# Attention scores in two strips of 64 rows, taken two units at a time

## What is computed

```
x = x + 0.5 * ffn(layernorm(x))        # top 2 of 8 experts, hidden width 352
x = x + attn(layernorm(x))             # 16 heads of 8 features
x = x + 0.5 * ffn(layernorm(x))

attn:  q, k, v = x @ qkv_w.T;  q, k = rope(q), rope(k)
       s = q @ k.T * 8 ** -0.5 + min(key - query, 0) * slope[head] * 8
       out = (softmax(s) @ v) @ proj_w.T + proj_b
```

## Time and profile before

| | |
|---|---|
| median of 3 runs | 501.61 us (497.75 to 501.74) |
| the profiled execution | 502.36 us, of which the span is 500.5 us |
| mean granted TensorE clock | 0.972 |
| busy share of PE, PEld, DVE, ACT, POOL | 88%, 73%, 64%, 50%, 47% |
| shares of the chain that ended last | PE 58%, DVE 8%, issue 7%, ACT 5%, POOL 4%, DMA 3% |

### The profile page before, as it was taken

The page is one execution under the profiler, slowest core; times in us unless marked ns, Lnnn a source line. Parts: engine busy times, 40 slices in busy tenths (PEclk is TensorE's granted clock), DMA queues, the critical chain, the costliest instruction groups (busy, mean ns, idle before and its releaser), DMA issues.

```text
span 500.5 us, 10906 instructions
## 1 busy us (share of the span) xinstructions
PE 439.6 (88%) x3447; PEld 367.2 (73%) x3447; DVE 318.6 (64%) x935; ACT 249.1 (50%) x585; POOL 236.9 (47%) x321
## 2 busy tenths in 40 slices
PE   1999989989889884998989898989788999999990
PEld 1878878888878663676867676767557988888880
DVE  3767869778556645384868585847436675545672
ACT  4745644364443534354565546454664554554441
POOL 7267796564523214034435253514254568643341
PEclk9999999999999989798999899999998999999996
DMA  9981121223220102121212111110022123223522
GB/s 245 284 116 55 48 75 45 79 71 97 70 60 24 43 22 54 33 65 34 55 53 54 45 48 40 45 43 22 7 87 64 53 67 112 59 60 96 149 79 79
DMA packets 50633, 35.51 MB, mean 71 GB/s; under 512 B 5754, under 2 KB 47706, under 8 KB 50538
## 3 DMA queue, kind: packets, MB, share of 16 engines
q1 hardware_dynamic: 45140, 23.90, 19.3%
q0 software_dynamic: 4784, 10.54, 6.3%
q10 hardware_dynamic: 656, 0.40, 0.3%
HBM read 15.37 MB, written 13.01 MB: 57 GB/s over the span
## 4 chain that ended last, share of the span: by engine, by line
PE 58%; DVE 8%; issue 7%; ACT 5%; POOL 4%; DMA 3%; ACTq 1%; SPq 1%; POOLq 0%; DVEq 0%
PE bank L1582 6%; PE bank L1485 5%; PE bank L1606 5%; PE bank L1621 5%; PE bank L1478 5%; PE bank L1467 4%; PE bank L1468 3%; PE bank L1469 3%; PE bank L1585 3%; PE bank L1586 3%; PE bank L1609 2%; PE bank L1610 2%; POOL yp L538 2%; PE bank L1457 2%; DVE nm L1260 2%
## 5 line engine op out<-in xcount | busy, mean ns | idle before, releaser
L538 POOL DMA_INDIRECT yp<-scr,dest x77 | 76.5, 994 | 90.2 <-ACT scr L768 63.1
L1260 DVE TENSOR_REDUCE nm<-bank 128x2 f32<-128x512 f32 x128 | 83.9, 685 | 46.6 <-PE bank L1586 45.1
L875 ACT ACTIVATE stage<-bank 128x512 f32<-128x512 f32 x128 | 75.2, 596 | 68.8 <-PE bank L1610 68.1
L1485 PE MATMUL bank<-wd,scr 128*128 (+1 forms) x462 | 64.2, 275 | 1.3 <-ACT scr L761 1.3
L1467 PE MATMUL bank<-wu,xbT 128*128 x154 | 62.3, 405 | 2.1 <-DVE xbT L1126 1.8
L1134 DVE COPY scr<-bank 128x256 f32<-128x256 f32 x77 | 32.5, 423 | 46.8 <-PE bank L1478 46.3
L1485 PEld LDWEIGHTS bank<-wd,scr 128*128 128x128 f32 (+1 forms) x462 | 60.0, 191 | 1.8 <-issue 1.7
L1582 PE MATMUL bank<-qk_rows 126*128 126x256 bf16 x256 | 51.4, 283 | 5.5 <-DVE nm L1260 5.5
L1606 PE MATMUL bank<-qk_rows 128*128 128x256 bf16 x256 | 50.9, 282 | 2.4 <-DMA qk_rows<-wd 2.0
L781 ACT ACTIVATE scr<-bank 128x352 f32<-128x352 f32 x77 | 35.7, 464 | 32.4 <-PE bank L1469 32.1
L1469 PE MATMUL bank<-wu,xbT 128*128 x154 | 50.2, 326 | 0.0
(11 more groups left out here) (218 smaller groups left out, 958.7 us busy)
## 6 DMA issues: line engine op xcount, KB each, us to landing
qk_rows<-lev SPq DMA_DIRECT2D x96, 64.0 KB
scr<-xs SPq DMA_DIRECT2D x77, 64.5 KB, 1.9
stage<-yp SPq DMA_DIRECT2D x8, 256.0 KB, 4.1
scr<-yp SPq DMA_DIRECT2D x6, 256.0 KB, 2.9
stage<-in_w SPq DMA_DIRECT2D x8, 176.0 KB, 3.7
stage<-in_v SPq DMA_DIRECT2D x8, 176.0 KB, 5.1
xs<-qk_rows SPq DMA_DIRECT2D x3, 451.5 KB, 11.1
yp<-scr,dest POOLq DMA_INDIRECT x77
```

The lines of the kernel that those rows point to most:

```text
L538: nc.gpsimd.indirect_dma_start(out=yp[PHASE[n]][:, :], out_offset=bass.IndirectOffsetOnAxis(ap=dest[:, n:n + 1], axis=0), in_=ysb[:, n % Y ...
L875: nc.scalar.activation(probs[:, g % RING, kt, 2 * (hp % 2):2 * (hp % 2) + 2, :], psS2[(b * 16 + j) % 3][:, :].rearrange("p (h n) -> p h n" ...
L1260: nc.vector.tensor_reduce(nm[:, qt, 2 * hp:2 * hp + 2], psS1[i % 2][:, :].rearrange("p (h n) -> p h n", h=2), AX.X, ALU.max, negate=True). ...
L1485: i = nc.tensor.matmul(ph[n % len(ph)][:, 3 * P:4 * P], hTs[0:w, n % 2, k * P:(k + 1) * P], wd[0:w, bass.ds(experts[n], 1), k, :].rearrang ...
```

## The change

The 62 to 64 meaningful rows are now packed at a step of 8 into a strip of 64 partitions. Even heads lie in rows 0 to 63, odd heads in rows 64 to 127, so `qs` and `ks` hold 8 heads a strip, side by side in one tile. `scores_1` and `scores_2` are called for two units at once: unit i is the lower strip, unit i+1 the upper one, in two PSUM banks, and their products alternate. The near triangle is contracted over 64 rows too, which needs a part 128 wide and a part 64 wide for each of high and low (`near`). `STRIP` is 64, `NEAR` is 192. The two units together have 12 products where they had 8.

```
-S1_SLOTS = [1, 1, 2, 2, 0, 1, 1, 2, 2, 2, 1, 1, 0, 0, 0, 0]
-S1_LATE = [0, 0, 0, 1, 1, 1, 2, 2, 2, 2, 2, 2, 1, 0, 0, 0]
+S1_SLOTS = [2, 0, 2, 2, 0, 2, 2, 0, 2, 2, 0, 2, 0, 0, 0, 0]
+S1_LATE = [0, 0, 0, 2, 0, 2, 2, 0, 2, 2, 2, 2, 2, 0, 0, 0]
...
+            def near(o, i, c, col):
+                for parts in (near_hi, near_lo):
+                    for half in range(2):
+                        w = slice(half * P, P + half * STRIP)
...
+                        for strip in range(2):
+                            rows = slice(strip * STRIP, (strip + 1) * STRIP)
+                            m = nc.tensor.matmul(o[strip]..., idn_r[rows, to:to + P], parts[i][rows, 2 * c:2 * c + 2, w], ...)
...
             def scores_1(b, i):
...
                 if i >= 2:
-                    pe.wait_ge(max_found, b * 16 + i - 1)
-                o = psS1[i % 2]
-                for j in range(2):
-                    h = 2 * hp + j
-                    nc.tensor.matmul(o[:, j * N:(j + 1) * N], qs[b % RING][0:S1_ROWS, h, ...],
-                                     ks[b % RING][0:S1_ROWS, h, :], start=(j == 0), stop=False)
+                    pe.wait_ge(max_found, b * 16 + i)
+                for a in range(2):
+                    for strip in range(2):
+                        rows = slice(strip * STRIP, strip * STRIP + S1_ROWS)
+                        nc.tensor.matmul(psS1[strip][:, a * N:(a + 1) * N], qs[b % RING][rows, 2 * c + a, ...],
+                                         ks[b % RING][rows, 2 * c + a, :], start=(a == 0), stop=False)
+                near(psS1, 0, c, qt * P)
...
             def scores_2(b, j):
-                if n >= 3:
-                    pe.wait_ge(exp_done, n - 2)
-                o = psS2[n % 3]
+                if n >= 2:
+                    pe.wait_ge(exp_done, n - 1)
+                o = [psS2[(n + strip) % 3] for strip in range(2)]
```

The calls: PE makes a pair of `scores_2` units at every even slot and a pair of `scores_1` units at the slots with a 2. The maxima are split on DVE ahead of the transposes; ACT makes one copy and issues its two transfers one after the other, ahead of `ln2`:

```
-            def max_low(b):
-                dve.wait_ge(ml_hi, b + 1)
-                nc.vector.tensor_tensor(ml[:, 1, :], psS1[0][0:H, 0:N], ml[:, 0, :], ALU.subtract)
+            def max_split(b):
+                dve.wait_ge(max_found, b * 16 + 16)
+                nc.vector.tensor_copy(nm_hi[:, :, :], nm[:, :, :])
+                dve.wait_ge(nm_step, 3 * b + 1)
+                nc.vector.tensor_copy(nm_parts[:, :, 0, :], nm_hi[:, :, :])
+                nc.vector.tensor_tensor(nm_parts[:, :, 1, :], nm[:, :, :], nm_hi[:, :, :], ALU.subtract)
...
+            def max_rows(b):
+                act.wait_ge(mT_full, b + 1)
+                nc.scalar.activation(ml, psS1[0][0:2 * H, 0:N], copy)
+                act.wait_ge(ml_done, b + 1)
+                for strip in range(2):
+                    at = strip * STRIP + S1_ROWS
+                    act.dma_start(qs[b % RING][at:at + 2, :, :], ml[strip::2, :])
```

More of the change, by code:

```diff
@@ L489, in stack @@
-            def stack(b):
-                for level in range(3):
-                    for i in range(3 - level):
-                        stack_level(b, level, i)
+            def stack(b, pairs):
+                for t in pairs:
+                    x, y = PAIRS[t]
+                    if t == 0 and b >= RING:
+                        sp.wait_ge(s2_full, 16 * (b - RING + 1))
+                    sp.wait_ge(split_step, b * 5 + (2, 4, 5)[max(x, y)])
+                    for strip in range(2):
+                        sp.dma_start(qk_s[b % RING][strip * STRIP + t:(strip + 1) * STRIP:SPREAD],
+                                     lev[strip::2, x:4 + y:3 + y - x, :]).then_inc(stack_landed[b % RING], 16)
@@ L634, in _ @@
             add_ffn_bias(0, 0)
-            pool.wait_ge(const_landed, 16 * 3)
-            nc.gpsimd.tensor_scalar(slope8[:, :], slope8[:, :], 8.0, None, ALU.mult).then_inc(slope_done, 1)
+            pool.wait_ge(const_landed, 16 * 2)
+            for strip in range(2):
+                at = slice(strip * STRIP, (strip + 1) * STRIP)
+                if strip:
+                    pool.wait_ge(bias_added, 1)
+                nc.gpsimd.tensor_scalar(slope_near[at, :], slope8[at, strip::2], 8.0, None, ALU.mult).then_inc(slope_done, 1)
+            pool.wait_ge(slope_done, 2)
             pool.wait_ge(numbered, 3)
@@ L647, in _ @@
             pool.wait_ge(tab[0], 10)
-            for i in range(2 * RING):
+            for i in range(RING):
                 nc.gpsimd.memset(qk_f[:, i * 2048:(i + 1) * 2048], 0.0).then_inc(zero_done, 1)
@@ L1565, in qk @@
                 i.then_inc(qk_full, 1)
+            def near(o, i, c, col):
+                for parts in (near_hi, near_lo):
+                    for half in range(2):
+                        w = slice(half * P, P + half * STRIP)
+                        to = STRIP * ((half == 0) == (i == 1))
+                        at = col + (STRIP if half and i else 0)
+                        for strip in range(2):
+                            rows = slice(strip * STRIP, (strip + 1) * STRIP)
+                            m = nc.tensor.matmul(o[strip][:, :].rearrange("p (h n) -> p h n", h=2)[:, :, at:at + P // (1 + half)],
+                                                 idn_r[rows, to:to + P], parts[i][rows, 2 * c:2 * c + 2, w],
+                                                 start=False, stop=(half == 1 and parts is near_lo))
+                            if half == 1 and parts is near_lo:
+                                m.then_inc((s1_full, s2_full)[i], 1)
             def scores_1(b, i):
-                qt, hp = i // 8, i % 8
+                qt, c = i // 8, i % 8 // 2
                 if i == 0:
@@ L1673, in _ @@
                 for s in range(16):
-                    scores_2(b, s)
+                    if s % 2 == 0:
+                        scores_2(b, s)
                     if b + 1 < B:
-                        for i in s1_units(b, s):
+                        for i in s1_units(b, s)[::2]:
                             scores_1(b + 1, i)
```

208 lines of the change are left out of this document (103 added, 105 removed).

## The result

The changed kernel takes **536.4 us** (median of 4 runs, 535.3 to 537.9) where the kernel before takes 500.6 (4 runs, 497.8 to 501.7): a ratio of 1.073, 95% interval 1.067 to 1.079. The profiled execution took 537.9 us with a span of 536.1; the mean granted TensorE clock is 0.916 (before 0.972). The forecast was 521.5, between 502 and 548.

The account below looks back on a forecast made before the run. PE was taken to bound the batches before, DVE with its answers afterwards. Batches 2 to 4 +10.7, 5 and 6 +5.7, batch 1 +3, batch 0 -1, early blocks +1.5: +19.9 us, a median of 521.5, range 502 to 548.

Parts of the forecast that it names:

- What bounds the kernel before: Steady batches: PE, 88% busy, bounds them; DVE reduces one unit while PE makes the other.
- The price of a pair: Two units of scores on PE: 0.70 us in strips, where full-height products take 0.93.
- loads take turns: Rival, chance 0.20: loads of the two strips can't overlap on PE, a pair costs 1.0 us, 545 in all.
- nothing overlaps: Rival, chance 0.07: the strips on PE don't overlap at all, a pair costs 1.38 us, 576 in all.
- half price: Rival, chance 0.15: the strips' products on PE take half the units' time, 0.465 us a pair, 504 in all.
- Changes of mode: Entering another tiling on PE costs about 0.1 us; 16 more changes in a steady batch, 1.6 us.
- The added wait: Next pair waits for both maxima; called the deciding term, 2.22 us between neighbouring pairs with nothing between.
- The walk: DVE followed through a steady batch, pairs 0 to 7 and its end: 29.5 us, against 25.3 in batch 4.
- The clock: Rival within the likeliest case's upper end, no own chance: PE's waits bring 1.2 GHz stretches, 1 to 3 us a batch, up to 535.
- tail of 9.0: End of a steady batch, after pair 7's maxima to the next batch's first maximum: 9.0 us, before 7.0.
- The smaller terms: Outside steady batches: early blocks +1.5 us, batch 0 -1, batch 1 +3, batch 7 0, stack transfers 0.
- PE stays the bound: Rival, chance 0.13: DVE's answers hide behind PE's other steps, 2.1 us less in each of seven batches, 487.

Follow-up runs that it names:

- experiment 1: Kernel before with only the changed kernel's `scores_1` slots and its wait for both maxima of a pair, full-height products: 501.4 us, ratio 1.0036.
- experiment 7: Kernel before with the changed kernel's `scores_1` slots and wait, and `scores_2` two units at a time at even slots, full-height products: ratio 1.007.
- experiment 10: Changed kernel with the split ahead of `combine`, filler products in PE's idle stretches, and `ln2` between the two row transfers: 515.7 us, ratio 1.029.
- (9): Changed kernel with the split ahead of `combine` and filler products ahead of the layer norm transposes and the logits: 516.1 us, ratio 1.030.
- experiment 3: Changed kernel with 10 needless products ahead of the layer norm transposes and 5 ahead of the logits: 522.2 us, ratio 1.047.
- experiment 11: Changed kernel with split ahead, filler, `ln2` between transfers, and `rotate_sin` behind the next pair's maxima, ACT's parts a slot later: 512.1 us, ratio 1.022.

## Why the prediction was right in direction and short in size

Batch 4 in steps, each from a trace:

| kernel | batch 4, us | step |
|---|---|---|
| before | 25.3 | |
| the wait and its slots alone (1) | 26.4 | +1.1 |
| `scores_2` in pairs too, no strips (7, another chip) | 26.7 | +0.3 |
| strips, filler, split ahead, `ln2` between (10) | 27.75 | +1.0 |
| the same, both row transfers ahead of `ln2` (9) | 28.1 | +0.35 |
| the same, `combine` ahead of the split (3) | 28.8 | +0.7 |
| changed kernel | 31.8 | +3.0, the clock |

To see where in the batch the strips cost time, cut it at the first maximum of pair 0 and at that of pair 7. DVE in experiment 3, strips at full clock, at these two places and at the next batch's pair 0:

```profile
294.80 1.28 DVE L1283 TENSOR_REDUCE nm<-bank 128x2 f32<-128x512 f32 x2
...
313.19 1.29 DVE L1283 TENSOR_REDUCE nm<-bank 128x2 f32<-128x512 f32 x2 [0.89 <-PE bank L1604]
...
323.56 1.28 DVE L1283 TENSOR_REDUCE nm<-bank 128x2 f32<-128x512 f32 x2
```

From pair 0 to pair 7 it takes 18.4 us; experiment 7, the same order with full-height products, takes 18.6 (296.31 to 314.88), and experiment 1 takes 18.4. Behind pair 7 it takes 10.4, and the other two 8.2 and 8.1. So under this wait the strips won next to nothing between the pairs (0.2) and lost nothing there. The end of the batch is 2.2 us longer in experiment 3 than in experiment 7: 0.7 by `combine` ahead of the split, 0.35 by the two transfers, and some 1.2 by the split, the filler and the rest, which wasn't taken apart. Experiment 7 ran on the other chip, but experiment 1, which didn't, has the same two stretches within 0.2.

- **What bounds the kernel before.** PE, which is right for the steady batches: shorter maxima left batch 4 at 25.1 us (25.3).
- **The price of a pair**, 0.70: measured 0.64 to 0.65. Its working stands only in part: a single strip costs the same 0.64, so the two strips run side by side, loads included, and one strip's six loads and products set the time. The rivals *loads take turns* (1.0) and *nothing overlaps* (1.38) are out, as is *half price* (0.465). The Trainium skill, TensorEngine Tiling (Array Packing), Key Properties, says that tiles load and multiply in parallel; the trace agrees (0.64 for one strip or two). Its Theoretical Speedup of up to 2x isn't reached here: 0.93 to 0.64 is 1.45. By columns alone it would be 1.6 (2048 to 1280) and not 2, because each near table needs 384 columns a strip where the full array needed 256.
- **Changes of mode**, 0.1 each: measured 0.09, from strips to the full array.
- **The added wait.** The walk holds span by span. With the clock kept up (experiment 3) pairs 0 to 1 took 3.4 (put at 3.7), the plain hops 2.17 to 2.18 (2.22), the rotation 3.9 (4.0), the attention add 2.4 (2.36), 6 to 7 2.1 (2.45), and the end of the batch from pair 7 on 10.4 (10.3): 28.8 us for 29.5. But "this is the term that decides" was too much. The same wait and order on full-height products cost 1.4 us a batch, and from pair 0 to pair 7 they take as long as with strips. Under the wait the gain of the strips, 16 pairs at 0.29 us less each, hardly shows: 0.2 us in all between pair 0 and pair 7. A kernel with strips and without this wait at otherwise the same order was not run, so what the wait costs there is not measured.
- **The clock** is the term that was mis-sized. The prediction had it as a rival, "1 to 3 us a batch", and in the sum at nothing. It cost 3.0 us in batch 4, 4.3 in batch 2, and 14 in all (536.4 against 522.2 with the filler). The forecast's 521.5 is thus the sum of a kernel whose clock stays up. That the two agree to 0.7 us is in part luck: against experiment 3's trace, the sum had batches 2 to 6 3.2 us too high and what lies before slot 1 of batch 1 3.1 too low. The place was right only in part. The prediction sought the fall behind the waits for maxima of 1.5 us in mid-batch. It is there in batch 2 (1.40) and in experiments 10 and 11. But in every batch from 1 to 6 the clock is low at the end, where in batch 4 0.9, 1.9 and 1.0 us of idle time follow each other (in batch 2 it fell after the first of them), and the prediction had that idle time in its own tail of 9.0.
- **The smaller terms.** The early blocks and batch 0: +3.7 to slot 1 of batch 1, where +0.5 was put (the first value products of batch 0 come 5.6 later, 179.8 for 174.2, and 1.9 are won back). PE waits 2.00 us for the stack's transfers before its first pair, which the prediction costed at 0 in the attention and didn't look at in the early blocks, and three times 1.77 for maxima (1.17 before, 0.6 more, as forecast). Batch 1 +2.3 for 3. The end +2.1 for 0: in batch 7 `scores_2` runs in pairs too, 17.9 us for 16.5.
- **PE stays the bound** (487) failed at the very sum of spans that it named. Of what the prediction said would show: DVE's idle pieces of 0.9 are there, PE waits for maxima 2.7 us in batch 4 and not 4 to 5, and slot 1 of batches 4 and 5 lies 31.8 us apart and not 29 to 30; the difference is the clock's 3.0. One of its signs of being wrong came true: PE waits elsewhere than at `max_found` and `nm_step`, for 1.9, 1.0 and 0.5 us behind ACT in batch 4 (before 1.0 and 0.5), and it is these waits that the low clock follows.

The row where the mis-sized term could be seen beforehand was at hand: the value products at 1.83 behind an idle stretch of 3.2 us. Where a walk lengthens idle stretches of PE, the sum has to say what the products behind them cost at the low level too, with such a row as the price.

## What to carry to other kernels

Two strips are worth their time only if what waits for a pair can use both results at once. Here an engine takes them one by one and the next pair waits for it, and a pair that is 0.29 us cheaper saved 0.2 us a batch between the pairs. A strip without a partner costs more than a full-height unit. Before an engine is made faster, see whether it is kept busy afterwards: PE lost some 3 us a batch by a clock that fell behind the idle time that the change had made, and products that nobody reads, in exactly those gaps, gave it back. A wait that looks like the deciding one in a walk is to be weighed against the same walk with the old products: here that order cost 1.4 us, where the changed kernel lost 6.5.

## What the runs showed of the hardware

- Products in two strips of 64 rows overlap fully when they are issued in turns, loads of the stationary operand included: 0.64 to 0.65 us for 12 products with 12 loads, and the same for 6 in one strip alone. They overlap in part even when one strip's six stand ahead of the other's: 0.85.
- Going from strips to the full array costs 0.09 us.
- The granted clock went to 0.50 (1.2 GHz) at the end of a batch, behind idle stretches of which none was over 1.9 us, and value products and logits took nearly twice their time. Work in the gaps kept it at 1.00. In experiment 3 it delayed nothing behind it; in experiment 10 the transposes behind it came 0.3 us later.
- The clock also went to 0.50 in mid-batch, behind a wait of 1.40 us (batch 2 of the changed kernel, two batches of experiment 10) and behind waits of 0.83 and 0.74 us (two batches of experiment 11). In other batches of the same kernels the same waits left it at 1.00 (1.38 in batch 4 of the changed kernel). What decides between them was not found.
